# A transformer block with its guard moved off VectorE, four score banks at the end, and two chunk streams 23 steps apart

## What is computed

```python
x = x + 0.5 * ffn(layernorm(x))
x = x + attn(layernorm(x))
x = x + 0.5 * ffn(layernorm(x))

def bitnet_linear(x, weight, scale_param):          # q, k, v and the output projection
    s = maximum(mean(abs(weight), axis=1), 1e-8)
    y = einsum('bsi,oi->bso', x, sign(weight / s[:, None])) * (s * scale_param)
    return nan_to_num(y, nan=0.0, posinf=1e6, neginf=-1e6)
# attn: 32 query heads and 8 key/value heads of 16, softmax(q k / 4) v, output projection
# ffn:  x @ W_base.T + b_base + 2 * sum over the two best of 8 experts of w * (x @ A_e.T) @ B_e.T
```

## Time and profile before

| | us |
|---|---|
| median of 3 runs (1208.24 to 1212.01) | 1210.61 |
| the profiled execution | 1210.39 |
| its span | 1208.6 |
| PE busy, share of the span | 1081.1, 89% |
| VectorE | 876.0, 72% |
| ScalarE | 708.4, 59% |
| GpSimd | 306.2, 25% |
| first exponential of the loops starts at | 238.26 |

### The profile page before, as it was taken

How to read it: one execution, slowest core, us unless ns; L and a number is a source line. 1 busy time by engine, 2 the same in 40 slices (tenths; PEclk the granted TensorE clock), 3 DMA queues, 4 the chain that set the end, 5 groups by cost and what they waited for, 6 DMA issues and landing times.

```text
span 1208.6 us, 19276 instructions
## 1 busy us (share of the span) xinstructions
PE 1081.1 (89%) x5944; PEld 491.6 (41%) x5944; DVE 876.0 (72%) x1259; ACT 708.4 (59%) x1313; POOL 306.2 (25%) x527
## 2 busy tenths in 40 slices
PE   1877676699999999999999999999999999999857
PEld 1666564334433342334333433443343334333336
DVE  3676869677787778787778777868886787782164
ACT  2343432365776667676667666756765676668511
POOL 4134345610241033141032104210510241032010
PEclk9997989699999999999999999999999999999968
DMA  7012133121121111300300021103101200200300
GB/s 244 18 53 83 53 92 103 33 69 36 32 55 32 38 30 46 77 25 25 77 24 24 24 79 31 34 26 77 27 24 47 54 24 24 77 6 6 87 0 36
DMA packets 87331, 59.03 MB, mean 49 GB/s; under 512 B 44144, under 2 KB 73328, under 8 KB 87280
## 3 DMA queue, kind: packets, MB, share of 16 engines
q1 hardware_dynamic: 87280, 58.39, 16.7%
HBM read 37.64 MB, written 20.32 MB: 48 GB/s over the span
## 4 chain that ended last, share of the span: by engine, by line
PE 73%; DVE 16%; ACT 5%; issue 3%; POOL 1%; DMA 1%; SPq 0%; DVEq 0%; ACTq 0%; POOLq 0%
PE ps_out L1226 19%; PE ps_score L1214 18%; PE ps_max L1193 15%; PE ps_fill L1151 6%; DVE neg_max L1015 3%; PE ps_fill L1178 2%; DVE neg_max L1073 2%; ACT probs L786 2%; PE ps_fill L1124 2%; PE ps_out L1151 2%; PE ps_fill L1155 1%; DVE xt_l L968 1%; DVE zd L927 1%; PE ps_fill L1136 1%; PE ps_max L1207 1%
## 5 line engine op out<-in xcount | busy, mean ns | idle before, releaser
L786 ACT ACTIVATE probs<-ps_score 128x512 f32<-128x512 f32 x1024 | 555.8, 595 | 275.1 <-PE ps_score L1214 273.5
L1015 DVE TENSOR_REDUCE neg_max<-ps_max 128x1 f32<-128x1024 f32 x480 | 571.4, 1218 | 175.7 <-PE ps_max L1193 174.6
L1214 PE MATMUL ps_score<-qst,kst 99*128 99x512 bf16 x1024 | 319.8, 386 | 11.0 <-ACT probs L786 7.8
L1193 PE MATMUL ps_max<-kst,qst 96*128 96x512 bf16 x1024 | 290.0, 384 | 20.7 <-DVE neg_max L1073 12.4
L1226 PE MATMUL ps_out<-probs,v_ring 128*32 128x512 f32 x2048 | 274.5, 608 | 0.0
L1214 PEld LDWEIGHTS ps_score<-qst,kst 99*128 99x128 bf16 x1024 | 88.1, 97 | 287.6 <-ACT probs L786 243.5
L1193 PEld LDWEIGHTS ps_max<-kst,qst 96*128 96x128 bf16 x1024 | 89.2, 98 | 137.5 <-DVE neg_max L1073 21.8
L307 POOL TENSOR_TENSOR wait_pad<-wait_pad 1x1 bf16<-1x1 bf16 x75 | 16.3, 217 | 395.9 <-DVE neg_max L1015 335.0
L1226 PEld LDWEIGHTS ps_out<-probs,v_ring 128*32 128x32 f32 x2048 | 40.4, 108 | 90.7 <-issue 90.3
L1124 PE MATMUL ps_fill<-ident,xn 128*128 128x128 f32 x192 | 32.1, 292 | 37.1 <-ACT xn L735 25.7
L735 ACT ACTIVATE xn<-xc,ln_shift,rstd 128x512 f32<-128x512 f32 x48 | 38.1, 810 | 41.0 <-POOL ln_shift L574 40.5
(11 more groups left out here) (202 smaller groups left out, 1276.5 us busy)
## 6 DMA issues: line engine op xcount, KB each, us to landing
qst<-q_dram SPq DMA_DIRECT2D x192, 64.0 KB, 2.2
q_dram<-zm SPq DMA_DIRECT2D x24, 256.0 KB, 2.6
kst<-k_dram SPq DMA_DIRECT2D x192, 32.0 KB, 2.1
xc<-x SPq DMA_DIRECT2D x8, 512.0 KB, 3.9
x_dram<-xc SPq DMA_DIRECT2D x8, 512.0 KB, 2.9
xc<-x_dram SPq DMA_DIRECT2D x8, 512.0 KB, 4.1
out<-xc SPq DMA_DIRECT2D x8, 512.0 KB, 2.8
att_dram<-att SPq DMA_DIRECT2D x31, 128.0 KB, 2.0
```

The lines of the kernel that those rows point to most:

```text
L786: act.activation(probs[:, kt % 2, j, :], ps_score[j % 2][:, :], ACT.Exp, scale=1.0 / HD ** 0.5).then_inc(probs_ready, 1)
L1015: dve.tensor_reduce(neg_max[:, uu % 2, t:t + 1], ps_max[max_slot(uu, pos)][:, :, :], AXY, ALU.max, negate=True).then_inc(max_read, 1)
L1193: last = pe.matmul(ps_max[slot][:, half, :], qst[0:SR, r, j, q * P:(q + 1) * P], kst[0:SR, r, half * 512:half * 512 + 512], start=True, st ...
L1214: pe.matmul(ps_score[j % 2][:, :], kst[0:SR + PARTS, uu, kt * P:(kt + 1) * P], qst[0:SR + PARTS, uu, j, :], start=True, stop=True).then_in ...
```

## The change

Five things are changed.

1. The front guard has another form. ScalarE evicts the product to `zd`, and a further copy writes its negative to `z` (`zpos`). GpSimd clamps both with min 0, max -BIG, subtracts the second result from the first, and writes the mask as value x 0. VectorE keeps the predicated copy. `FRONT_ON_DVE` is empty, so this holds for all four pairs.
2. `SLOT_LAG` is 23, not 9. The list ALONE has 348 steps as before; `START` moves from 299 to 310, and the 33 uses stand on the last 38 steps instead of the last 49.
3. The split's subtractions are made in pieces of 512, 512 and 256 columns.
4. The weights' conversions on ScalarE stand behind T1b of chunk A0, the low parts on VectorE behind T1bl of A0, the scales and PE's sum behind FFb3 of A0.
5. In units 30 and 31, where no maxima are made any more, score tiles 2 and 3 go to the `ps_max` bank pair that is free.

```diff
-SLOT_LAG = 9
+SLOT_LAG = PAIR_PERIOD // 2
...
-FRONT_ON_DVE = ("clamp", "sum")
+FRONT_ON_DVE = ()
...
+        zpos = z
...
+        def four_score_banks(i, uu):
+
+            return isinstance(i, int) and UB * i + uu >= NU - 2
+
+        def score_bank(i, uu, j):
+
+            if four_score_banks(i, uu) and j >= 2:
+                return ps_max[1 - turn_slot(uu, True)][:, j - 2, :]
+            return ps_score[j % 2][:, :]
...
+                if ch.front:
+                    gp.wait_ge(negated[s], ch.n * 3 + piece + 1)
+                    gp.tensor_scalar(zneg[s][:, cols], zd[s][:, cols], 0.0, -BIG, ALU.min, ALU.max).then_inc(clamped[s], 1)
+                    gp.tensor_scalar(zpos[s][:, cols], z[s][:, cols], 0.0, -BIG, ALU.min, ALU.max).then_inc(clamped[s], 1)
+                    return
...
+                if ch.front:
+                    gp.tensor_tensor(zpos[s][:, cols], zneg[s][:, cols], zpos[s][:, cols], ALU.subtract).then_inc(clamp_sum[s], 1)
+                    return
...
-                gp.tensor_scalar(zneg[s][:, cols], z[s][:, cols], 0.0, 0.0, ALU.mult, ALU.add).then_inc(guard_step[s], 1)
+                value = zd[s] if ch.front else z[s]
+                gp.tensor_scalar(zneg[s][:, cols], value[:, cols], 0.0, 0.0, ALU.mult, ALU.add).then_inc(mask_ready[s], 1)
...
+                    for a0 in range(0, KQ, 512):
+                        piece = slice(a0, min(a0 + 512, KQ))
+                        rest = kq[:, piece] if k == 1 else parts[s][:, 2, piece]
+                        last = gp.tensor_tensor(rest, kq[:, piece], parts[s][:, k - 1, piece], ALU.subtract)
+                    last.then_inc(part_rest[s], 1)
...
+                if pos in ("C0", "C1", "C2") and ch.front:
+                    k = int(pos[1])
+                    cols = slice(512 * k, 512 * k + 512)
+                    bnk, reads = ch.bank(("VK", "Q0", "Q1")[k])
+                    act.wait_ge(filler_read[bnk], reads + 1)
+                    act.activation(z[s][:, cols], zd[s][:, cols], ACT.Copy, scale=-1.0).then_inc(negated[s], 1)
...
-                act.activation(probs[:, kt % 2, j, :], ps_score[j % 2][:, :], ACT.Exp,
+                act.activation(probs[:, kt % 2, j, :], score_bank(i, uu, j), ACT.Exp,
...
+                if item[0].n == 0 and item[1] == "T1b" and item[0].slot == 0:
+                    ffn_weights()
...
-                if step[0] == "G" and ch.front:
-                    dve.wait_ge(clamp_sum[s], ch.sum0 + (k + 1))
-                    dve.tensor_scalar(mask, z[s][:, cols].bitcast(I32), INF_BITS, INF_BITS, ALU.bitwise_and,
-                                      ALU.bitwise_xor).then_inc(guard_step[s], 1)
...
-                        dve.copy_predicated(zd[s][:, cols], mask, z[s][:, cols]).then_inc(guard_step[s], 1)
+                        dve.copy_predicated(zd[s][:, cols], mask, zpos[s][:, cols]).then_inc(guard_step[s], 1)
...
-                if item[0].n == 0 and item[0].slot == 1 and item[1] == "LN1c":
+                if item[0].n == 0 and item[0].slot == 0 and item[1] == "T1bl":
                     ffn_weights()
-                if item[0].n == 0 and item[0].slot == 1 and item[1] == "FFa3":
+                if item[0].n == 0 and item[0].slot == 0 and item[1] == "FFb3":
                     attn_scales()
...
             def score(i, uu, kt, j):
-                if not isinstance(i, int) or 32 * (UB * i + uu) + 4 * kt + j >= 2:
+                if four_score_banks(i, uu) and kt == 0 and j >= 2:
+                    pe.wait_ge(max_read, max_use(i, 1, 16) + 1 if uu == 2 else turn_use(i, 2, True) + 1)
+                elif four_score_banks(i, uu) and kt > 0:
+                    pe.wait_ge(probs_ready, i * (32 * UB) + (32 * uu + 4 * kt + j - 3))
+                elif not isinstance(i, int) or 32 * (UB * i + uu) + 4 * kt + j >= 2:
                     pe.wait_ge(probs_ready, i * (32 * UB) + (32 * uu + 4 * kt + j - 1))
```

## The result

The changed kernel takes 1229.05 us (median of 4 runs, 1226.23 to 1230.87) where the kernel before takes 1211.31 beside it: a ratio of 1.0149, with a 95% interval from 1.0129 to 1.0169. It is slower, by 17.7 us; the forecast was 7. The profiled execution took 1230.87 us. First the page after: its span, the busy times, and the granted clock in 40 slices.

The account below looks back on a forecast made before the run. Neither PE nor VectorE on average: they take turns in the alone phase; afterwards the fixed order would set the period. Alone phase +9.7, bodies +0.5, units -3.0 made +7.2: 1217.5 us; own range 1209 to 1227, 8 in 10 1196 to 1231.

Parts of the forecast that it names:

- The start: Run's beginning to stream A's first V and K product: 58.5 us for 67.5, with weights ready earlier.
- The four halves: Alone phase, A0's to A2's V and K product: four half periods of 32.5 us, 130 for 120.0.
- The guard on GpSimd: Front guard in the alone phase: 3.2 us a piece, clamps 0.63, subtraction 1.3, test 0.61; VectorE relieved.
- rival 3: GpSimd becomes the bound: guard pieces 5.8 us, halves of 37, 1235 us; chance 0.07.
- The walk: Steps followed from A's V and K product to B's, half a period: 30.7 us at full clock.
- The mechanism named: Alone phase: S1 and S2 (split subtraction, cast) of one stream ahead of the other's normalisation; decides above 31 us a half.
- Last stretch: From A2's V and K product to the first exponential: 59.5 us for 50.8.
- Units 30 and 31: Last units, with four score banks: scores done earlier, -3.0 us, bounds 0 and -3.7.
- bodies: Loop bodies 0 and 1: ScalarE copies beside a busy PE, less mask work on VectorE; +0.5 us, between 0 and +3.
- 1 and 2: Rivals: streams flow past each other, halves 28.5 us, 1199.5 (chance 0.25); nothing in total, halves 30.7, about 1209.5 (chance 0.15).
- The signs named beforehand: Profile after: w_rep at 26 to 28 us, clamps 0.6, second xn half awaiting S2, PE half clock once a half.

## Why the prediction was right or wrong

The sign was right and the size was less than half: +7.2 us forecast, +17.7 measured. The measured 1229.05 us lies above the forecast's own range (1209 to 1227) and inside the range for 8 in 10, whose upper end is 1231.

Two terms of the sum failed. The start was to give 9.0 us and gave 3.6. The four halves were to cost 10.0 and cost 18.4. On the chain of a half two terms make up the difference: PE's half clock, which the prediction put at 1.8 us and which was 2.6, and the time in which VectorE and GpSimd hold each other, which it put at nothing, though the earlier trace rows showed such a hold, and which was 1.6. The other terms held. That both big parts lose, the guard and the distance, is shown by the runs with each alone; which waits make a half at 23 steps is only read from the chain. By its steps, against the sum of 1217.6 us for the profiled execution, which took 13.3 more:

**Start: 5.4 us under.** w_rep of the first chunk was ready at 25.8 us, as forecast (26). Behind it the chain after shows slow matmuls and the scales in the way (start, duration, what), with the window of the first of them below:

```profile
25.36 0.44 DVE w_rep L925
...
27.11 5.49 PE ps_fill L1176 x12
32.60 1.08 PE ps_fill L1180 x3
...
40.45 2.68 DVE zm L868
43.18 5.41 PE ps_score L1123 x8
```

```profile
27.00:33.00 6.00, 5.89 (x14) 4.62 (x15) 1.09 (x3) 5.06 (x5) 0.00 (x0) 1.00 0.00 0
```

The 12 feed-forward matmuls take 2.80 us at full clock (2.10 for 9), and the 8 of sum_o 3.70 in the kernel before. Together with 1.08 for 0.70 that is 4.8 us, where the prediction had 1.3 for the clock: 3.5 of the 5.4, by the chain. For sum_o the granted clock was 0.50 from 44 to 46 us. For the feed-forward matmuls the profile shows 1.00, and only their length (5.49 for 2.80) speaks for half speed. Nor is the clock shown to be the whole cause: with the old guard and 9 steps A0's product came at 63.95 us too, and there the profile shows 1.00 throughout. That run does show that neither guard nor distance is to blame for the start. The term was seen and mis-sized; 1.9 us are not accounted for.

**The guard on GpSimd: prices right, sign of the move wrong.** These groups by form, up to 262 us, have one clamp at 0.63 us (the other has the same), the subtraction at 1.30, the test at 0.72, and the predicated copy:

```profile
L616 POOL TENSOR_TENSOR zm<-zm 128x512 f32<-128x512 f32 x18 | 23.5, 1303 | 1.5
...
L641 POOL TENSOR_SCALAR zm<-zd 128x512 f32<-128x512 f32 x18 | 12.9, 716 | 1.6
L602 POOL TENSOR_SCALAR zm<-zd 128x512 f32<-128x512 f32 x18 | 11.4, 633 | 49.2 <-ACT zm L796 49.2
```

```profile
L952 DVE COPY_PREDICATED zd<-zm 128x512 f32<-128x512 int32 x18 | 18.0, 1001 | 3.7 <-POOL zm L641 3.7
```

So rival 3 with its 1.93 us is out, and the split's pieces took 2.9 for 3.3 to 3.4. But the prediction counted the move as relief for VectorE, whose 28.5 busy us of 29 it had seen, and did not ask what such a stretch becomes on the slower engine. The run at 9 steps shows it: a chain of 36 us on GpSimd where VectorE had been nearly full for 30. At 23 steps the move costs 4 us in all by the medians (two banks in both), and 0 to 4 us a period by the profiles.

**Halves: 34.6 for 32.5.** The walk (30.7) had the right steps in the right order. The rest of a half in the chain above is (a) PE at half clock: A's transposes and B's last feed-forward piece 3.45 us, then T2b 1.13, then the V and K product with the two transposes in it 3.11, where the halves with full clock have 2.07, 0.45 and 2.55: 2.6 us; (b) VectorE and GpSimd holding each other: the test 0.98 for 0.62, the first small operation of the normalisation 0.76 for 0.23, the predicated copy 1.41 for 0.65, 1.6 us; less 0.4 for the shorter S1. The prediction added 1.8 for (a) and nothing for (b). That gives 3.8, the 34.5 of this half against the 30.7 walked. But this is a reading of one chain and not what a half would gain: the run with unread matmuls, the split and the bias additions moved got back 1.3 to 2 us of a half, since other chains end little sooner and a part of (b) was still there.

**The mechanism named was not the one.** The prediction had the price in S1 and S2 ahead of the other stream's second xn half. These do stand on the chain (4.1 us of a half), but without S1 on GpSimd a half was not shorter by more than two profiles of the same alone phase differ. That the order at 23 steps costs was right: the distance alone makes a period 5 to 8 us longer. None of the single waits that were moved carries it; which set of the order's waits does is open.

**Last stretch** 59.8 for 59.5, and its working holds too: the first reduction starts 9.8 us after A2's product (9.2), and 28 reductions stand ahead of the last predicated copy, which ends after 54.3 (53.3). **Units 30 and 31** and bodies gained 3.3 us for 2.5: right, within what one profile tells. A window over the 47.5 us of units 30 and 31 (PE busy 43.74, before 46.58 in 50.3) says the same:

```profile
1113.00:1160.50 47.50, 43.74 (x263) 17.47 (x263) 8.96 (x29) 38.13 (x74) 7.66 (x17) 1.00 0.16 37
```

**Rivals.** 1 and 2 are out: their walk ends at 30.7 or below, and even with both reliefs no mean of four halves came under 32.6. What the text had against 1, the order on the engines, fits: no engine was full, and the halves were long. The signs named beforehand came out as written for w_rep, the clamps, the wait for S2 and the half clock; those for the period (63 to 66 us) and the first exponential (244 to 252) did not.

## What to carry to other kernels

Before a stretch without a gap is moved from one engine to another, add up what the new engine then does in that stretch, at its own prices and with what it had there already: being idle on average says nothing of it. Where two streams alternate in a fixed order, measure the period for several distances: here the first period was 66, 60, 62 and 65 us for 5, 9, 13 and 23 steps with the old guard (the split is on VectorE in the first three and on GpSimd in the last; at 9 steps that made 59.5 and 59.1), and no argument from busy shares gave that order. And where a change has several parts, run the small ones alone: here the two parts that looked like details were worth 9 us together, and the big ones lost 27.

## What had not been expected of the hardware

An operation of VectorE or GpSimd beside one of the other lasts up to thirteen times as long as alone: a 4-column cast 2.18 us for 0.17, a 128x2 operation on GpSimd 0.76 for 0.23 beside a predicated copy and 1.38 beside a subtraction of 1280 columns. The mean predicated copy rose from 0.80 us to 1.00 with the change.

And PE's lower level (granted 0.50, which is 1.2 GHz) was worth less than the slow matmuls on the chain suggest. PE had it in every half of the changed kernel's alone phase, after stretches in which it mostly waited (busy 0.73 of the 3 us from 114.9 to 117.9); two of the stretches at this level, in windows of PE alone (stretch, length, PE busy, granted clock, DMA, GB/s):

```profile
121.00:130.00 9.00, 5.82 (x25) 0.50 0.05 13
154.00:165.00 11.00, 7.62 (x33) 0.50 0.05 16
```

22 unread matmuls a chunk brought the clock of a period from 0.73 to 0.91, but the time only from 1229.1 to 1225.8 us, with intervals that overlap.
